# A masked attention stage with its values as the stationary operand, and spare products on PE ahead of two expert stages

## The chip, the cores and the metric

One core of a Trainium2 chip runs the whole program. The metric is the device time of one execution in microseconds (us), lower is better. Three executions of the kernel before took 1061.87, 1064.99 and 1067.60 us; their median is 1064.99 us.

## The reference

The input is 16 sequences of 128 tokens with 256 features, and a context tensor of the same shape. Four residual updates follow each other:

- `x += q + tril(c cT) q` with `q = layernorm(x)` and the context `c`, per sequence.
- A latent attention and a mixture of 8 experts. The tokens are normalized, brought down to 128 latent features, and split into 16 heads of 8 features. Rotated queries and keys give causal scores, and `attn = softmax(scores)`, `o = attn @ v`, `x + o @ w_up`. Each token then goes to 2 of 8 experts of width 512.
- A cross attention of 16 heads of 64 features, scaled by tanh of a gate.
- A mixture of 16 experts of width 256 (2 per token), and a shared expert of width 512 that all tokens use.

The change concerns the product `attn @ v` of the second item, with the division by the softmax's sums, and the beginnings of the two expert stages.

## The kernel before, in words

The kernel writes each engine's instructions in an order that a small planner fixes at build time. `latent_phases`, `expert_phases`, `cross_phases` and `shared_phases` (lines 161 to 360) declare phases: an engine, an assumed cost in ns, the phases that must come first, the PSUM banks that it holds, and a due time. `Plan.order` (lines 104 to 151) plays these costs forward and takes the phase whose start plus due is least; the table `LEAD` (lines 74 to 81) shifts single phases in it. The engines then run these orders in sequence, each instruction waiting for semaphores, so a phase that waits holds all that is behind it on its engine.

**The first stage** handles 16 blocks (one per sequence), pipelined over each other. For one block:

- PE forms the masked context product and applies it (`ctx`, `q1`), transposes the normalized tokens (`hnT`), and makes latent features (`c`) and queries, keys and values (`qkv`). ScalarE's `qkv_e` (line 998) copies the values into a ring of four tiles `v_`, each 16 heads times 9 columns. The ninth column of each head is a one, so that the product with the probabilities also gives their sum.
- `s` (line 701) writes scores of all 16 heads in four PSUM banks: a bfloat16 product that puts the causal mask there (line 708, 512 columns), then products of 32 rows (line 717) that lie in four different strips of the array.
- VectorE takes the maxima (line 1319), ScalarE the exponentials (line 1023), PE transposes the probabilities group by group (`pT`, line 727), ScalarE copies them out (`pT_e`, line 1030).
- `pv` (lines 730 to 738) multiplies: for each of the 16 heads the 128 by 128 transposed probabilities are the stationary operand, and the head's 9 value columns move.
- VectorE's `nrm0` (line 1322) takes reciprocals of the 16 sums per token and multiplies. The result has tokens on the partitions, so PE transposes it once more (`oT`, line 740), ScalarE copies it (`oT_e`, line 1032), and `up` (line 745) multiplies by `w_up`.
- The rest is a normalization and the router: transposes (`tT`), logits (`log`), counts (`cnt`) on PE, and small steps on VectorE (`ra`, `rb`), and GpSimd scatters the tokens to DRAM, sorted by expert (line 1780).

A float32 matmul appears in the profile as two LDWEIGHTS and MATMUL pairs, so the 16 products of `pv` are 32 records of each.

**The expert stages** (`r` = 0 and 1) walk over tiles of 128 sorted rows: SyncE loads a tile's rows (line 1863), `xT` (line 773) transposes them, `gate_up` (line 780) and `down` (line 796) multiply by the expert's weights. Before the first tile, SyncE and ScalarE write padding rows (lines 1845 and 1053 ff.). The first tile's `xT` waits for its rows, and PE with it.

Of the kernel before, what the change touches and what calls it, by code (L numbers as in the profile page):

```python
# [26 lines left out]
TRASH = 2 * NB * 128  # L27
KB = 256
# [12 lines left out]
def constants():  # L41
# [33 lines left out]
    "Q": 100, "SD": 600, "btg": 1000, "c_e": -100, "cpow": 800, "epow": 700, "exp0": -100, "ga0": 1200,  # L75
    "gates_a": -200, "gates_e": -1300, "kml": 1700, "kwl": -1600, "load_kv": -2400, "load_q": -700,
# [84 lines left out]
def latent_phases(p):  # L161
# [3 lines left out]
    for b in range(NB):  # L165
        def add(engine, ns, key, *after, banks=(), **kw):
            p.add(engine, ns, key, *after, banks=banks, due=20 * b, **kw)
# [15 lines left out]
        add("PE", 650, ("qkv", b), ("c_e", b), banks=[(misc, ("qkv_e", b))])  # L183
        add("ACT", 500, ("qkv_e", b), ("qkv", b), ("pv", b - 4), ("qkT", b - 2))
# [13 lines left out]
        add("PE", 3600, ("pv", b), *[(f"pT_e{g}", b) for g in range(4)], banks=[("pv", ("onrm", b))])  # L198
# [192 lines left out]
def program(nc, a, out):  # L391
    with ExitStack() as ctx:
# [96 lines left out]
        def emptied(*key, i=0):  # L489
            bk, n = USE[key][i]  # L490
            return freed[bk], n + 1
# [79 lines left out]
        o_ = lat.ring(2, 128)  # L571
        v_ = lat.ring(4, 16 * 9)
        rs_ = lat.ring(6, 8)
        sm_ = lat.ring(2, 64)
# [51 lines left out]
        def unit(s):  # L626

            return s // 8, s // 4 % 2, s // 2 % 2, s % 2

# [28 lines left out]
        def tensor(pe):  # L658
# [71 lines left out]
            def pv(b):  # L730
                vacant(pe, "pv", b)
                for g in range(4):
                    pe.wait_ge(*emptied(f"pT{g}", b))
                    for n in range(4):
                        h = 4 * g + n
                        i = pe.matmul(ps("pv", b)[:, h * 9:h * 9 + 9], pt_[g][:, n * 128:n * 128 + 128],  # L736
                                      v_[b % 4][:, h * 9:h * 9 + 9], start=True, stop=True)
                i.then_inc(*fills("pv", b))

            def oT(b):  # L740
                vacant(pe, "oT", b)
                pe.wait_ge(*emptied("pv", b))
                pe.transpose(ps("oT", b)[:, 0:128], o_[b % 2], ident).then_inc(*fills("oT", b))
# [195 lines left out]
            for phase, *at in ORDER["PE"]:  # L939
                if phase in ("pT0", "pT1", "pT2", "pT3"):  # L940
                    pT(at[0], int(phase[2]))
                elif phase == "EC":
                    cnt(at[0], 1)
                elif phase in ("gate", "up"):
                    gate_up(*at, phase)
                else:
                    {"ctx": ctx, "q1": q1, "hnT": hnT, "c": c, "qkv": qkv, "qkT": qkT, "s": s, "pv": pv, "oT": oT, "wup": up, "tT": tT,
                     "log": log, "cnt": cnt, "xT": xT, "down": down, "K": K, "V": V, "Q": Q, "S": scores, "T": T,
                     "PV": PV, "W": W, "NT": NT, "ET": ET, "EL": EL, "SG": SG, "SD": SD}[phase](*at)
# [25 lines left out]
        def scalar(act):  # L975
# [22 lines left out]
            def qkv_e(b):  # L998
                act.wait_ge(*full("qkv", b))
                if b >= 4:  # L1000
                    act.wait_ge(*full("pv", b - 4))
                v = v_[b % 4].rearrange("p (h d) -> p h d", d=9)
                if b < 4:
                    act.wait_ge(sem("sum_columns"), 4)
# [26 lines left out]

            def oT_e(b):
                act.wait_ge(*full("oT", b))
                if b >= 2:
                    act.wait_ge(*full("wup", b - 2))
                act.copy(oT_[b % 2], ps("oT", b)[:, 0:128]).then_inc(*frees("oT", b))
# [179 lines left out]
            for phase, *at in ORDER["ACT"]:  # L1216
# [4 lines left out]
                else:  # L1221
                    {"setup_a": setup, "hnT_e": hnT_e, "c_e": c_e, "qkv_e": qkv_e, "qkh": qkh, "oT_e": oT_e,
# [5 lines left out]
        def vector(v):  # L1228
# [4 lines left out]
            def setup():  # L1233
# [7 lines left out]
                for t in v_:  # L1241
                    v.memset(t.rearrange("p (h d) -> p h d", d=9)[:, :, 8:9], 1.0).then_inc(sem("sum_columns"), 1)
# [79 lines left out]
            def nrm0(b):  # L1322
                v.wait_ge(*full("pv", b))
                pv = ps("pv", b)[:, 0:144].rearrange("p (n d) -> p n d", n=16)
                sums = sm_[b % 2][:, 16:32].rearrange("p (n o) -> p n o", o=1)
                v.reciprocal(sums, pv[:, :, 8:9]).then_inc(dv, next_step("dve"))
                then()
                if b >= 2:
                    v.wait_ge(*full("oT", b - 2))
                v.tensor_tensor(o_[b % 2].rearrange("p (n d) -> p n d", n=16), pv[:, :, 0:8],  # L1330
                                sums.broadcast_to([128, 16, 8]), ALU.mult).then_inc(*frees("pv", b))
# [638 lines left out]
```

## Time and profile before

| | |
|---|---|
| median of three runs | 1064.99 us |
| the profiled execution, its own time | 1073.64 us |
| its span, first to last instruction | 1071.8 us |
| mean granted TensorE clock | 0.905 |
| busy: PE, its weight loads, DVE, ACT, POOL | 90%, 83%, 69%, 57%, 25% |
| first stage, from first to last `pv` | 53.7 to 254.1 us |
| first expert stage begins on PE | 281.3 us |
| second expert stage begins on PE | 876.6 us |

PE is the TensorE matmul, PEld its weight loads, DVE VectorE, ACT ScalarE, POOL GpSimd, SP SyncE. The granted clock is a share of full speed, where 0.50 is 1.2 GHz and 1.00 is 2.4 GHz.

### The profile page before, as it was taken

How to read it: one execution, taken by the hardware profiler on the slowest of the kernel's cores; microseconds unless marked ns; L12 is line 12 of the kernel's file. 1: busy time of each engine (PE TensorE's matmuls, PEld its weight loads, DVE VectorE, ACT ScalarE, POOL GpSimd, SP SyncE). 2: the span in 40 equal slices, each digit the busy share in tenths (PEclk: the TensorE clock that was granted, in tenths of full speed). 3: DMA queues.
4: the chain of work that ended last, by engine and by line, in shares of the span. 5: the costliest groups of instructions: out<-in, count | busy, mean ns of one | idle time of the engine just before them, and what ended most of it. 6: DMA issues, size and time to landing. Idle time of an engine off the chain costs nothing.

```text
span 1071.8 us, 23321 instructions
## 1 busy us (share of the span) xinstructions
PE 968.7 (90%) x7674; PEld 886.3 (83%) x7674; DVE 736.0 (69%) x2033; ACT 614.6 (57%) x1690; POOL 269.6 (25%) x323
## 2 busy tenths in 40 slices
PE   4799999997499999997899999999998829999994
PEld 3488888886499999996789899989887729999994
DVE  5876676654466776665899878576775528888836
ACT  1465666663366666666476486575775317767510
POOL 2544454543000000001735412101111103333300
PEclk7976787876699999998999999999998959999998
DMA  9600000000331111113111100000130853333242
GB/s 385 277 12 21 11 22 21 21 21 31 80 134 55 51 51 51 54 37 113 50 31 46 35 22 21 11 12 21 39 126 16 370 143 91 91 100 95 76 168 69
DMA packets 37317, 82.49 MB, mean 77 GB/s; under 512 B 5488, under 2 KB 28784, under 8 KB 35920
## 3 DMA queue, kind: packets, MB, share of 16 engines
q1 hardware_dynamic: 29760, 61.63, 16.6%
q0 software_dynamic: 6864, 18.85, 5.3%
q8 instruction: 63, 1.03, 0.4%
q10 hardware_dynamic: 576, 0.53, 0.2%
q14 instruction: 54, 0.44, 0.1%
HBM read 55.95 MB, written 25.04 MB: 76 GB/s over the span
## 4 chain that ended last, share of the span: by engine, by line
PE 76%; issue 6%; DVE 5%; DMA 4%; POOL 3%; ACT 2%; SPq 2%; ACTq 0%; DVEq 0%; another core or an unknown queue 0%; POOLq 0%
PE ps L792 17%; PE ps L654 8%; PE ps L656 8%; PE ps L655 8%; PE ps L736 6%; PE ps L727 4%; PE ps L877 3%; PE ps L856 3%; PE ps L866 3%; PE ps L935 2%; PE ps L708 2%; POOL yt_dram L1801 2%; PE ps L717 1%; DMA CT<-in_ctxT 1%; PE ps L692 1%
## 5 line engine op out<-in xcount | busy, mean ns | idle before, releaser
L654 PE MATMUL ps<-BIGR 128*128 128x256 f32 (+1 forms) x826 | 258.6, 313 | 7.6 <-DVE BIGR L1555 3.3
L792 PE MATMUL ps<-BIG 128*128 128x128 f32 x2000 | 254.5, 277 | 1.7 <-DVE BIG L1550 1.0
L792 PEld LDWEIGHTS ps<-BIG 128*128 128x128 f32 x2000 | 240.5, 194 | 3.5 <-DVE BIG L1550 2.4
L656 PE MATMUL ps<-BIGR 128*128 128x256 f32 x762 | 216.0, 283 | 0.0
L654 PEld LDWEIGHTS ps<-BIGR 128*128 128x128 f32 x826 | 158.5, 192 | 15.1 <-issue 9.3
L655 PE MATMUL ps<-BIGR 128*128 128x256 f32 (+1 forms) x570 | 168.9, 296 | 0.0
L656 PEld LDWEIGHTS ps<-BIGR 128*128 128x128 f32 x762 | 145.4, 191 | 0.0
L1080 ACT COPY BIG<-BIG 128x512 f32 (+1 forms) x86 | 70.1, 815 | 110.1 <-PE ps L792 73.9
L1543 DVE TENSOR_TENSOR BIGR<-BIG,BIGR 128x512 fp32r<-128x512 f32 (+1 forms) x86 | 80.4, 934 | 47.0 <-ACT BIGR L1089 46.8
L655 PEld LDWEIGHTS ps<-BIGR 128*128 128x128 f32 x570 | 109.2, 192 | 1.9
L1174 ACT ACTIVATE BIG<-ps,sm 128x128 f32<-128x128 f32 x256 | 91.5, 386 | 11.3 <-DVE sm L1644 11.1
L1793 POOL DMA_INDIRECT BIG<-ys_dram,YI x32 | 31.8, 994 | 238.1 <-DMA ys_dram<-BIG 230.4
L1780 POOL DMA_INDIRECT xs_dram<-TT,PI x64 | 65.2, 1018 | 95.7 <-DVE PI L1400 85.6
L1728 POOL TENSOR_TENSOR st<-st,CS 128x1 f32<-128x1 f32 (+1 forms) x64 | 43.4, 679 | 179.8 <-DVE st L1255 179.2
L1801 POOL DMA_INDIRECT yt_dram<-BIG,IX x47 | 48.8, 1039 | 123.1 <-DVE BIG L1563 120.7
L1089 ACT CAST BIGR<-BIG 128x512 fp32r (+1 forms) x86 | 69.4, 807 | 16.5 <-DMA BIG<-in_wd 11.1
L736 PEld LDWEIGHTS ps<-BIG 128*128 128x128 f32 x512 | 70.2, 223 | 3.3 <-issue 3.0
L655 PE MATMUL ps<-CTR,BIGR 128*128 128x256 f32 x256 | 72.9, 285 | 0.0
L736 PE MATMUL ps<-BIG 128*128 128x9 f32 x512 | 70.9, 280 | 1.8 <-ACT BIG L1030 1.5
L1550 DVE TENSOR_TENSOR BIG<-ps,BIG 128x256 f32<-128x256 f32 (+1 forms) x86 | 46.7, 543 | 34.2 <-PE ps L792 34.1
L1023 ACT ACTIVATE BIG<-ps,BIG 128x128 f32<-128x128 f32 x256 | 69.6, 432 | 0.0
L1641 DVE TENSOR_REDUCE sm<-ps 128x4 f32<-128x512 f32 x64 | 44.0, 687 | 32.0 <-PE ps L856 32.0
(221 smaller groups left out, 1998.5 us busy)
## 6 DMA issues: line engine op xcount, KB each, us to landing
BIG<-in_wd SPq DMA_DIRECT2D x2, 4096.0 KB, 35.5
BIG<-in_wgu SPq DMA_DIRECT2D x1, 6144.0 KB, 18.9
BIG<-xs_dram SPq DMA_DIRECT2D x47, 129.5 KB
BIG<-xs_dram SPq DMA_DIRECT2D x39, 128.0 KB
ys_dram<-BIG SPq DMA_DIRECT2D x39, 128.0 KB, 1.7
BIG<-yt_dram SPq DMA_DIRECT2D x16, 256.0 KB, 5.5
xs_dram<-zero SPq DMA_DIRECT2D x20, 129.5 KB, 7.1
X<-in_x SPq DMA_DIRECT2D x4, 512.0 KB, 8.6
```

The source lines that it names most:

```text
L654: pe.matmul(o, l[0], r[0], start=start, stop=False)
L655: pe.matmul(o, l[0], r[1], start=False, stop=False)
L656: return pe.matmul(o, l[1], r[0], start=False, stop=stop)
L736: i = pe.matmul(ps("pv", b)[:, h * 9:h * 9 + 9], pt_[g][:, n * 128:n * 128 + 128], v_[b % 4][:, h * 9:h * 9 + 9], start=True, stop=True)
L792: i = pe.matmul(o[:, c * 128:(c + 1) * 128], wt[:, at:at + 128], x[:, k * 128:(k + 1) * 128], start=k == 0, stop=k == 1)
L1023: i = act.activation(p_[g][:, at], ps("s", b, i=g)[:, at], ACT.Exp, bias=sm[:, 4 * g + n:4 * g + n + 1])
L1080: act.copy(W_[r][j % 2][:, n:2 * n], WGU[:, bass.ds(e * (2 * n) + n, n)]).then_inc(S["gu_upper"], 1)
L1089: act.copy(D_[j % len(D_)][:, 0:n], WD[:, bass.ds(e * n, n)]).then_inc(S["down_hi"], 1)
L1174: i = act.activation(xp_[s % 4][:, at], ps("S", s // 2, i=s % 2)[:, at], ACT.Exp, bias=sm[:, 4 + n:5 + n], accum_out=sm[:, 8 + n:9 + n])
L1543: v.tensor_tensor(wd[:, n:2 * n], WD[:, bass.ds(e * n, n)], wd[:, 0:n].bitcast(F32), ALU.subtract).then_inc(S["down_lo"], 1)
L1780: pool.indirect_dma_start(XS, bass.IndirectOffsetOnAxis(ap=PI[:, b, k:k + 1], axis=0), TT[tile_of(r, b)][:, :], None).then_inc(sem(f"scatt ...
L1801: pool.indirect_dma_start(YT, bass.IndirectOffsetOnAxis(ap=IX[:, j % 4:j % 4 + 1], axis=0), Y_[1][j % 3], None).then_inc(sem(f"results_pla ...
```

## The change

`pv` is turned round: a head group's values, padded to windows of 32 columns in which only one head's 8 columns are not zero, are the stationary operand, and the transposed probabilities move, 128 columns each. Four heads accumulate in one 32 by 128 piece of PSUM, and the four groups g lie at partitions 32g. A second set of 16 products has fixed tiles of ones as stationary operand and gives the sums, already spread over the partitions of each head. That makes 32 products for 16, all of form 128x32 with 128 moving columns, and the result comes out transposed, so `oT` and `oT_e` go. `nrm0` takes the reciprocal of 128 by 128 sums rather than of 128 by 16. `qkv_e` copies the values in four pieces. The ring of values has three tiles rather than four.

Before the first `xT` of the expert stages, PE does 40 (r = 0) and 24 (r = 1) bfloat16 products of 512 columns into the bank of `xT`, which then overwrites them. Assumed costs, some orderings and the table `LEAD` of the planner change as well, so the order of phases on every engine may change in all stages.

```diff
+VPAD = 88
+FILL = (40, 24)
 LEAD = {
-    "Q": 100, "SD": 600, "btg": 1000, "c_e": -100, ...
+    "ET_e": -300, "Q": 100, "SD": 600, "ah": -100, "btg": 1700, ...
-        add("PE", 650, ("qkv", b), ("c_e", b), banks=[(misc, ("qkv_e", b))])
-        add("ACT", 500, ("qkv_e", b), ("qkv", b), ("pv", b - 4), ("qkT", b - 2))
+        add("PE", 650, ("qkv", b), ("c_e", b), ("pv", b - 3), banks=[(misc, ("qkv_e", b))])
+        add("ACT", 600, ("qkv_e", b), ("qkv", b), ("pv", b - 3), ("qkT", b - 2))
-            add("PE", 440, (f"pT{g}", b), (f"exp{g}", b), banks=[("pT", (f"pT_e{g}", b))])
+            add("PE", 440, (f"pT{g}", b), (f"exp{g}", b), *[(f"pT{n}", b - 1) for n in range(4)], banks=[("pT", (f"pT_e{g}", b))])
-        add("PE", 3600, ("pv", b), ...)
-        add("DVE", 450, ("onrm", b), ("pv", b), ("oT", b - 2))
-        add("PE", 120, ("oT", b), ("onrm", b), banks=[(misc, ("oT_e", b))])
-        add("ACT", 170, ("oT_e", b), ("oT", b), ("wup", b - 2))
-        add("PE", 430, ("wup", b), ("oT_e", b), banks=[(misc, ("r", b))])
+        add("PE", 1800, ("pv", b), ...)
+        add("DVE", 560, ("onrm", b), ("pv", b), ("wup", b - 2))
+        add("PE", 430, ("wup", b), ("onrm", b), banks=[(misc, ("r", b))])
+        VAT, VWIN = (0, 48, 72, 32), (0, 40, 56, 8)
             def pv(b):
+
                 vacant(pe, "pv", b)
                 for g in range(4):
                     pe.wait_ge(*emptied(f"pT{g}", b))
+                if b == 0:
+                    pe.wait_ge(sem("sum_columns"), 8)
+                for x in range(2):
                     for n in range(4):
-                        h = 4 * g + n
-                        i = pe.matmul(ps("pv", b)[:, h * 9:h * 9 + 9], pt_[g][:, n * 128:n * 128 + 128],
-                                      v_[b % 4][:, h * 9:h * 9 + 9], start=True, stop=True)
+                        for g in range(4):
+                            w = v_[b % 3][:, VPAD * g:VPAD * g + VPAD] if x == 0 else ones_
+                            i = pe.matmul(ps("pv", b)[32 * g:32 * g + 32, 128 * x:128 * x + 128],
+                                          w[:, VWIN[n]:VWIN[n] + 32], pt_[g][:, n * 128:n * 128 + 128],
+                                          start=n == 0, stop=n == 3)
                 i.then_inc(*fills("pv", b))
-            def oT(b):
-                ...
             def up(b):
-                pe.wait_ge(*emptied("oT", b))
+                pe.wait_ge(*emptied("pv", b))
+            def keep_busy(bank, n):
+
+                for _ in range(n):
+                    pe.matmul(bank[:, :].rearrange("p (n t) -> p n t", n=4), identb[:, :],
+                              negb[:, :].rearrange("p (o t) -> p o t", o=1).broadcast_to([128, 4, 128]),
+                              start=True, stop=True)
             def xT(r, j):
                 vacant(pe, "xT", r, j)
+                if j == 0:
+                    keep_busy(ps("xT", r, j), FILL[r])
                 pe.wait_ge(sem(f"rows_loaded{j % 3}"), 16 * (rows_before(r, j) + 1))
             def qkv_e(b):
-                if b >= 4:
-                    act.wait_ge(*full("pv", b - 4))
-                v = v_[b % 4].rearrange("p (h d) -> p h d", d=9)
-                act.copy(v[:, :, 0:8], ps("qkv", b)[:, 256:384].rearrange("p (h d) -> p h d", d=8))
+                if b >= 3:
+                    act.wait_ge(*full("pv", b - 3))
+                else:
+                    act.wait_ge(sem("sum_columns"), 3)
+                v = v_[b % 3].rearrange("p (g c) -> p g c", g=4)
+                x = ps("qkv", b)[:, 256:384].rearrange("p (g n d) -> p g n d", g=4, n=4)
+                for n in range(4):
+                    act.copy(v[:, :, VAT[n]:VAT[n] + 8], x[:, :, n, :])
-            def oT_e(b):
-                ...
             def setup():
+                    v.memset(t, 0.0).then_inc(sem("sum_columns"), 1)
+                v.memset(ones_, 0.0).then_inc(sem("sum_columns"), 1)
+                ...
             def nrm0(b):
                 v.wait_ge(*full("pv", b))
-                v.reciprocal(sums, pv[:, :, 8:9]).then_inc(dv, next_step("dve"))
+                if b >= 2:
+                    v.wait_ge(*full("wup", b - 2))
+                o = oT_[b % 2]
+                v.reciprocal(o, ps("pv", b)[:, 128:256]).then_inc(dv, next_step("dve"))
                 then()
-                v.tensor_tensor(o_[b % 2]..., pv[:, :, 0:8], sums.broadcast_to([128, 16, 8]), ALU.mult)
+                v.tensor_tensor(o, ps("pv", b)[:, 0:128], o, ALU.mult).then_inc(*frees("pv", b))
```

## Rows read from the trace of the kernel before

**Rows 1.** The page: busy tenths, granted clock in 40 slices of the span

```profile
PE   4799999997499999997899999999998829999994
PEclk7976787876699999998999999999998959999998
```

**Rows 2.** Chain that ended last, share of the span by line

```profile
PE ps L792 17%; PE ps L654 8%; PE ps L656 8%; PE ps L655 8%; PE ps L736 6%; PE ps L727 4%; PE ps L877 3%; PE ps L856 3%; PE ps L866 3%; PE ps L935 2%; PE ps L708 2%; POOL yt_dram L1801 2%; PE ps L717 1%; DMA CT<-in_ctxT 1%; PE ps L692 1%
```

**Rows 3.** Stretches: us, busy of PE, PEld, DVE, ACT, POOL, granted clock, DMA share, GB/s

```profile
53.74:254.09 200.35, 197.90 (x1260) 168.14 (x1259) 133.10 (x437) 126.39 (x414) 89.62 (x117) 0.76 0.05 19
...
281.33:288.10 6.77, 6.26 (x28) 5.89 (x29) 0.00 (x0) 2.52 (x4) 0.00 (x0) 0.50 0.23 61
550.00:575.00 25.00, 24.83 (x238) 21.84 (x238) 23.40 (x64) 18.59 (x68) 10.68 (x13) 1.00 0.12 33
900.00:1000.00 100.00, 98.78 (x852) 96.85 (x850) 85.93 (x247) 71.29 (x177) 36.26 (x35) 1.00 0.32 96
...
876.60:882.10 5.50, 5.49 (x18) 4.78 (x19) 1.21 (x7) 0.37 (x1) 0.00 (x0) 0.51 0.17 50
```

**Rows 4.** Timeline of PE: start, us, group; a `pv`, and the last one

```profile
190.79 3.71 PE L736 MATMUL ps<-BIG 128*128 128x9 f32 x32
...
254.09 3.97 PE L736 MATMUL ps<-BIG 128*128 128x9 f32 x32
```

**Rows 5.** Timeline of PE: the cross attention's product of form 128x64

```profile
643.39 1.09 PE L877 MATMUL ps<-BIG 128*64 128x128 f32 x16
644.42 0.44 PE L866 MATMUL ps<-CS,BIG 128*128 128x128 f32 x2
```

**Rows 6.** Timeline of PE: products of 32 rows in four strips

```profile
200.79 0.97 PE L717 MATMUL ps<-BIGR 32*128 32x512 f32 x12
```

**Rows 7.** Reciprocals on VectorE, by line: duration ns min/median/max

```profile
L1649 DVE RECIPROCAL sm<-sm x64: 160/171/180, 534.9 to 820.1; 128x4 f32<-128x4 f32 x64
...
L1326 DVE RECIPROCAL BIG<-ps x16: 251/258/259, 58.2 to 258.1; 128x16 f32<-128x16 f32 x16
...
L1515 DVE RECIPROCAL GW<-GW x1: 352/352/352, 843.3 to 843.3; 128x32 f32<-128x32 f32 x1
```

**Rows 8.** Copies on ScalarE and the transpose that goes, by line

```profile
L1005 ACT COPY BIG<-ps x16: 245/265/293, 27.3 to 228.3; 128x128 f32<-128x128 f32 x16
...
L1036 ACT COPY BIG<-ps x16: 265/266/273, 63.4 to 259.3; 128x128 f32<-128x128 f32 x16
...
L743 PE MATMUL ps<-CS,BIG x16: 273/450/454, 63.1 to 258.8; 128*128 128x128 f32 x16
```

**Rows 9.** Chain in order of time and timeline: mask products, half and full clock

```profile
59.99 1.71 PE ps L708 x4
...
199.84 1.03 PE L708 MATMUL ps<-negb,identb 128*128 128x512 bf16 x4
```

**Rows 10.** Timeline of PE around the beginnings of the expert stages

```profile
268.17 0.17 PE L771 MATMUL ps<-mb,onesb 128*128 128x8 bf16 x1
281.33 0.45 PE L777 MATMUL ps<-CS,BIG 128*128 128x128 f32 x1 [12.99 <-DMA BIG<-xs_dram]
...
853.38 2.51 PE L935 MATMUL ps<-BIG,small 128*128 128x256 f32 x8 [2.55 <-DVE X L1702]
876.61 0.44 PE L777 MATMUL ps<-CS,BIG 128*128 128x128 f32 x1 [20.72 <-DMA BIG<-xs_dram]
```

**Rows 11.** Who waited, first stage: us in total, times, longest

```profile
POOL X L1768 <- DVE BIG L1339: 35.3, 13, 5.4
...
DVE BIG L1326 <- PE ps L736: 14.7, 13, 2.5
...
DVE BIG L1319 <- PE ps L717: 10.2, 9, 2.9
```

More of the change, by code:

```diff
@@ L74 @@
 LEAD = {
-    "Q": 100, "SD": 600, "btg": 1000, "c_e": -100, "cpow": 800, "epow": 700, "exp0": -100, "ga0": 1200,
-    "gates_a": -200, "gates_e": -1300, "kml": 1700, "kwl": -1600, "load_kv": -2400, "load_q": -700,
[4 rows of a table removed]
+    "ET_e": -300, "Q": 100, "SD": 600, "ah": -100, "btg": 1700, "c_e": 600, "cpow": 700, "epow": -700, "exp0": -100,
+    "ga0": 1300, "gates_a": -700, "kml": 200, "log": -300, "max": -3000, "max3": 100, "nh": -100, "nl": -200,
+    "owl": -1000, "pT0": 100, "pT3": -300, "pT_e0": -100, "pT_e1": 100, "pT_e3": -100, "pow3": -3700, "pro2": -300,
+    "qkT": -400, "qkh": -100, "qkl": -2200, "qkv_e": -200, "qw": 500, "qwl": 100, "r": -400, "ra1": -200,
+    "rope_p": 100, "route1": 1100, "sc0": 100, "sc1": -400, "sq": 700, "swh": -900, "tT": -1400, "tT_e": -100,
+    "te": 1500, "xbt": -100, "xh": 600, "xl": 100
 }
@@ L195, in latent_phases @@
             add("ACT", 1030, (f"exp{g}", b), (f"max{g}", b), (f"pT{g}", b - 1))
-            add("PE", 440, (f"pT{g}", b), (f"exp{g}", b), banks=[("pT", (f"pT_e{g}", b))])
+            add("PE", 440, (f"pT{g}", b), (f"exp{g}", b), *[(f"pT{n}", b - 1) for n in range(4)], banks=[("pT", (f"pT_e{g}", b))])
             add("ACT", 500, (f"pT_e{g}", b), (f"pT{g}", b), ("pv", b - 1))
-        add("PE", 3600, ("pv", b), *[(f"pT_e{g}", b) for g in range(4)], banks=[("pv", ("onrm", b))])
-        add("DVE", 450, ("onrm", b), ("pv", b), ("oT", b - 2))
-        add("PE", 120, ("oT", b), ("onrm", b), banks=[(misc, ("oT_e", b))])
-        add("ACT", 170, ("oT_e", b), ("oT", b), ("wup", b - 2))
-        add("PE", 430, ("wup", b), ("oT_e", b), banks=[(misc, ("r", b))])
+        add("PE", 1800, ("pv", b), *[(f"pT_e{g}", b) for g in range(4)], banks=[("pv", ("onrm", b))])
+        add("DVE", 560, ("onrm", b), ("pv", b), ("wup", b - 2))
+        add("PE", 430, ("wup", b), ("onrm", b), banks=[(misc, ("r", b))])
         add("DVE", 420, ("r", b), ("wup", b), ("xr", b - 2), ("tt", b - 2))
@@ L570, in program @@
         sq_ = lat.ring(1, D)
-        o_ = lat.ring(2, 128)
-        v_ = lat.ring(4, 16 * 9)
+        v_ = lat.ring(3, 4 * VPAD)
+        ones_ = lat.ring(1, VPAD)[0]
         rs_ = lat.ring(6, 8)
-        sm_ = lat.ring(2, 64)
+        sm_ = lat.ring(2, 16)
         ex0 = Space((120, BIGKB))
@@ L946, in tensor @@
                 else:
-                    {"ctx": ctx, "q1": q1, "hnT": hnT, "c": c, "qkv": qkv, "qkT": qkT, "s": s, "pv": pv, "oT": oT, "wup": up, "tT": tT,
+                    {"ctx": ctx, "q1": q1, "hnT": hnT, "c": c, "qkv": qkv, "qkT": qkT, "s": s, "pv": pv, "wup": up, "tT": tT,
                      "log": log, "cnt": cnt, "xT": xT, "down": down, "K": K, "V": V, "Q": Q, "S": scores, "T": T,
@@ L1030, in pT_e @@
                 act.copy(pt_[g], ps(f"pT{g}", b)[:, :]).then_inc(*frees(f"pT{g}", b))
-            def oT_e(b):
[L1033 to L1036, printed above, removed]
             def sq(b):
@@ L1221, in scalar @@
                 else:
-                    {"setup_a": setup, "hnT_e": hnT_e, "c_e": c_e, "qkv_e": qkv_e, "qkh": qkh, "oT_e": oT_e,
+                    {"setup_a": setup, "hnT_e": hnT_e, "c_e": c_e, "qkv_e": qkv_e, "qkh": qkh,
                      "sq": sq, "tT_e": tT_e, "pad_act": pad_act, "gates_e": gates_e, "wa": wa, "wdh": wdh, "xT_e": xT_e,
@@ L1241, in setup @@
                 for t in v_:
-                    v.memset(t.rearrange("p (h d) -> p h d", d=9)[:, :, 8:9], 1.0).then_inc(sem("sum_columns"), 1)
+                    v.memset(t, 0.0).then_inc(sem("sum_columns"), 1)
+                v.memset(ones_, 0.0).then_inc(sem("sum_columns"), 1)
+                v.wait_ge(sem("sum_columns"), 4)
+                for at in VAT:
+                    v.memset(ones_[:, at:at + 8], 1.0).then_inc(sem("sum_columns"), 1)
                 v.wait_ge(sem("consts_loaded"), 16)
@@ L1323, in nrm0 @@
                 v.wait_ge(*full("pv", b))
-                pv = ps("pv", b)[:, 0:144].rearrange("p (n d) -> p n d", n=16)
-                sums = sm_[b % 2][:, 16:32].rearrange("p (n o) -> p n o", o=1)
-                v.reciprocal(sums, pv[:, :, 8:9]).then_inc(dv, next_step("dve"))
+                if b >= 2:
+                    v.wait_ge(*full("wup", b - 2))
+                o = oT_[b % 2]
+                v.reciprocal(o, ps("pv", b)[:, 128:256]).then_inc(dv, next_step("dve"))
                 then()
[L1328 to L1331, printed above, removed]
+                v.tensor_tensor(o, ps("pv", b)[:, 0:128], o, ALU.mult).then_inc(*frees("pv", b))
             def r(b):
```

5 lines of the change are left out of this document (removed), and 4 rows, old and new, of the table LEAD.

## The prediction

> **What bounds the kernel now.** I read the page first. PE is busy nearly throughout, and its granted clock is at or close to full in the later stages but not in slices 2 to 11 [rows 1]. The chain that ended last is also mostly PE, and `pv`, line 736, has 6% of it [rows 2], some 64 us for 16 blocks of 9-column products. So the next view is the stretch from the first `pv` to the last: 200.35 us for 15 blocks, 13.36 us a block, with PE busy 197.90 us, or 99%, at a mean clock of 0.76, against DVE 133.10 and ACT 126.39 us [rows 3]. The reader should see two things there. PE alone sets the pace of the first stage. And it does so at a clock that is half of full for 48% of the time (0.76 is 0.52 at full and 0.48 at half). Freed of everything else, PE's work is 197.90 / 15 x 0.76 = 10.0 us of full clock a block; DVE's is 8.9 us, ACT's 8.4 us, POOL's 6.0 us. DVE waits for PE's products [rows 11], not the other way round. A faster `pv` is therefore worth its full price until DVE ends last, which is not far off.
>
> **`pv`.** Now 32 records take 3.71 us at mostly full clock [rows 4], about 112 ns each: with 9 moving columns that is the price of a 128-column weight load, not of a product. After, there are 64 records of 128 columns in a form with 32 weight columns. No row shows that form. The nearest is the cross attention's 128x64 form, whose products alternate between two halves of the array: 16 records in 1.09 us, of which the last one's latency of about 0.27 is tail, so 16 in about 0.87 [rows 5]. That is 54 ns a record, half of 112, so two column strips do work side by side. Four strips by rows do too: 12 records of 512 columns in 0.97 us [rows 6], where one after another they would need 12 x 0.217 = 2.6 (0.217 per 512 columns, from (1.03 - 0.38) / 3, the mask products at full clock [rows 9]). The changed loop runs g innermost, so each product goes to another strip than the last. I take four strips side by side: 64 / 4 x 109 ns = 1.75 us, and 0.15 for starting, 1.9 us. The bounds are 1.75 and, if no strip overlaps, 64 x 109 = 7.0 us; 54 ns, as the row of two strips has it, gives 3.5. I take the lowest but for the start because both rows of strips show the full factor that their number allows. `oT` takes one more product of 0.11 us at full clock off PE. PE's work becomes 10.0 - 3.6 + 1.9 - 0.1 = 8.2 us of full clock a block.
>
> The Trainium skill (TensorEngine Tiling (Array Packing), Key Properties) speaks against this: changing the tiling mode drains the engine. Behind the 64-column products of this trace the next one starts 1.03 us after they began [rows 5], some 0.1 to 0.2 us later than without a gap; by the page with such a drain at both ends of 16 `pv` it would be at most 6 us of PE in all, in a stage where PE is then no longer last, so the sum stays.
>
> **The clock.** Half clock comes in each block now, in the stretches with `pv` and behind it, where the array moves 9 columns per weight load. After, `pv` moves 128 columns in four strips, and 8.2 us of dense work would lie in some 11 us. I take the clock as close to full, 0.93 or more. If it keeps falling, that is a rival.
>
> **DVE.** The reciprocal grows from 16 to 128 elements per partition. Between 4 and 32 elements it costs (352 - 171) / 28 = 6.5 ns an element, and 258 ns at 16 [rows 7]; so 258 + 112 x 6.5 = 0.98 us, 0.72 more a block. Its bounds are 0.3 (no dependence on size) and 1.2 us. The planner assumes 560 ns for the pair, which I do not follow. The multiplication has 128 x 128 elements before and after. DVE's work becomes 133.10 / 15 + 0.72 = 9.6 us a block. It is now the largest of all, so DVE ends last. What share can it reach? At its best it is busy 23.40 of 25 us, and over a long PE-bound stretch 85.93 of 100 [rows 3]. That gives 9.6 / 0.94 = 10.2 and 9.6 / 0.86 = 11.2 us a block. I take 11.2: the order of phases is laid out with a too small `onrm`, and PE and ACT are then at 73 to 80% too.
>
> **ACT.** Four copies of 128x32 for one of 128x128 in `qkv_e`: each between 0.20 and 0.265 [rows 8], so 0.5 to 0.8 us more, less 0.27 for `oT_e` [rows 8]: 8.8 us a block at most. Hidden behind DVE; if DVE were faster it would be next. The other edits cost nothing: the zeroing of the tiles in the setup lies behind the first loads; `qkv_e` waits for the `pv` of three blocks back, `nrm0` for the `wup` of two back, both a whole block early; and `pv` waiting for all four `pT_e` costs its pipeline at most the copy of one group, 0.6 us of latency, against the 0.7 us that `oT` with `oT_e` give back.
>
> **Sum of the first stage.** 15 x (13.36 - 11.2) = 32 us. Behind the last `pv` the stage is a chain of dependent steps: that `pv` itself shrinks from 3.97 us [rows 4] to about 2 us, `oT` with its copy goes, the longer reciprocal comes: 2 us more. Together 34 us.
>
> **The 40 products.** PE stands idle 12.99 us, from 268.3 until the first rows land, and then works at clock 0.50 for 6.77 us [rows 3, 10]. The idle is set by DMA and the queues that pad, which the products do not touch. One product costs 1.71 / 4 = 0.43 us at half and 0.217 at full clock [rows 9]. The clock rose after 5.5 and 6.8 us of work in the two stage beginnings [rows 3], so 13 to 16 products run at half and the rest at full: 11.3 to 12.0 us. They end a microsecond before the rows; if the clock does not rise they take 17.2 us and delay the stage by 4. Then the expert stage's first 6.77 us run at full clock and take about half: 3 us gained, with bounds from 4 lost to 3.4 gained.
>
> **The 24 products.** The last product ahead of the second stage ends at 855.9, the rows land at 876.6 [rows 10]. 24 products take 5.2 us at full and 10.3 at half clock, so they end by 866, and more than 10 us of idle follow, as in front of the first stage, where such an idle left the clock at half. I expect nothing from them, neither gain nor loss, and the 5.50 us at 0.51 [rows 3] stay.
>
> **The new orders** of the later stages I count as 0, between 4 us gained and 5 lost: PE is at 98% there already [rows 3]. Together -32 - 2 - 3 = -37 us: the profiled span of 1071.8 would become 1035, its time 1073.64 about 1037. It stands 8.65 us above the median of the runs, so from the median, 1064.99 - 37 = 1028 us.
>
> **Rivals.** A difference within 0.5%, 5 us, is no difference here.
>
> *The clock keeps falling.* The 16 transposes a block and the small router products stay, and between them PE now waits for DVE. With the mean clock still at 0.76, PE needs 8.2 / 0.76 = 10.8 us a block, on top of DVE's 9.6; two engines so close give 12 us: -20 - 2 - 3, 1040 us. For it: the half-clock share is now 48%. Against: what held the clock down was mostly `pv`. The Trainium skill (TensorE: Matmul & The Clock Gate, Part 4) says that transposes do not count as busy for the clock, which would make this case likelier.
>
> *The 64 pairs are paced by their issue.* A pair of weight load and product every 105 ns is what the densest stretch shows (238 in 25 us [rows 3]), though those are long products. By that bound `pv` takes 6.7 us, PE 13.0 at full clock, and the time falls only by 5 + 3: 1057 us. A short burst goes faster, 54 ns [rows 5], which gives 3.5 us, PE 9.8, DVE still last, about 1032. In between, 1040. The Trainium skill (same page, Back-to-back issue gap) gives about 81 ns for such pairs; by it `pv` would take 5.2 us, PE 11.5, and the time would be near 1038.
>
> *No strip overlaps* (the slower case). `pv` then takes 7.0 us of full clock, PE 10.0 - 3.6 + 7.0 - 0.1 = 13.3, already all of the present 13.36. With the clock at 0.9, since transposes and waits still lower it a little, it is 14.8 us a block: 15 x 1.4 = 21 us lost, 3 won back by the 40 products, 1083 us. It decides from a `pv` of about 6 us on. Against it stand both strip rows.
>
> *The stage is faster, the program is not.* What the first stage gains, an order in the later stages loses. That needs over 30 us there, where PE idles little.
>
> **How the numbers follow.** Forecast 0.60, clock falls 0.17, issue 0.13, lost later or nothing gained 0.05, slower 0.05. The first three are all faster by more than 0.5%: 0.90; within 0.5%: 0.05; slower: 0.05. The range: DVE at 94% gives 15 x 3.2 = 47 + 5, 1013, and 3 from the orders 1010; at the other end 12.4 us a block with nothing for the tail gives 1050. 1010 to 1050 leaves out the slower case and the worst of the issue case.
>
> **What would show it.** Right: 64 records of `pv` in about 2 us, spaced near 27 ns; reciprocals near 1 us; blocks 11.2 us apart; clock above 0.9 in the first stage; DVE busy 86% there; PE idle in it for the first time, waiting for DVE; first expert stage at clock 1.00 from its first product; second one still at half. Wrong: `pv` records 109 ns apart, a clock of 0.76 as now, a reciprocal of 0.3 us (then below 1015), or PE still at 99%.

## The result and the profile after

The changed kernel takes 1020.41 us (median of 4 runs, 1019.6 to 1025.98) against 1065.72 us of the kernel before: ratio 0.959, 95% interval 0.9547 to 0.9634. That is 45 us or 4.1% faster, inside the range of 1010 to 1050 and 8 us below the forecast of 1028. Its profiled execution has a span of 1018.3 us and a time of 1020.09 us.

The page of the changed kernel, its busy tenths and the granted clock, answers to [rows 1]:

```profile
PE   4788888878999999978999999999999759999994
PEclk7889999998999999988999999999999979999997
```

PE is now below 9 in slices 3 to 9 where it stood at 9, and the clock is at 9 in slices 4 to 9 where it moved between 6 and 8. The chain of the changed kernel answers to [rows 2]; the first stage's product, now line 744, has 2% of it, and two VectorE lines appear:

```profile
PE ps L805 18%; PE ps L657 9%; PE ps L659 9%; PE ps L658 9%; PE ps L869 3%; PE ps L890 3%; PE ps L879 3%; PE ps L948 2%; POOL yt_dram L1812 2%; PE ps L744 2%; PE ps L730 1%; DVE BIG L1340 1%; DMA CT<-in_ctxT 1%; PE ps L711 1%; DVE BIG L1332 1%
```

Stretches of the changed kernel, with the columns of [rows 3]: first to last `pv`, the first expert stage's first 6.8 us, the cross attention from the first expert stage's last gate to the last count, and the second expert stage's first 5 us:

```profile
51.70:219.70 168.00, 142.24 (x1735) 101.48 (x1735) 145.81 (x450) 123.82 (x445) 90.66 (x123) 0.97 0.07 22
243.60:250.40 6.80, 6.29 (x54) 6.08 (x55) 1.38 (x2) 3.68 (x6) 0.00 (x0) 1.00 0.30 79
445.30:791.60 346.30, 331.28 (x2931) 298.85 (x2930) 260.83 (x780) 231.29 (x771) 97.77 (x110) 0.98 0.15 51
826.00:831.00 5.00, 5.00 (x20) 4.28 (x21) 0.80 (x4) 0.37 (x1) 0.00 (x0) 0.59 0.19 52
```

The first line is the heart of it: 15 blocks in 168.00 us, 11.2 us each, at a clock of 0.97, with DVE busy 145.81 us, 87%. The time before split by stages, from the two profiled executions:

| stage | before, us | after, us | difference |
|---|---|---|---|
| start to the first `pv` | 53.7 | 51.7 | -2.0 |
| first `pv` to the last | 200.4 | 168.0 | -32.4 |
| last `pv` to the first expert stage | 27.2 | 23.9 | -3.3 |
| first expert stage, to its last gate product | 204.7 | 201.7 | -3.0 |
| cross attention, to the last count | 355.0 | 346.3 | -8.7 |
| to the second expert stage's first product | 35.6 | 34.4 | -1.2 |
| second expert stage and end | 195.2 | 192.3 | -2.9 |

Together -53.5 us, from a profiled execution of before that lay 8 us above the median. The split is that of two single executions; stages of the same code differ by some us from one profile to the next, as the experiments show.

The timeline of PE in the changed kernel shows one `pv`, and the last one:

```profile
148.51 1.95 PE L744 MATMUL ps<-BIG 128*32 128x128 f32 x64
...
219.67 1.95 PE L744 MATMUL ps<-BIG 128*32 128x128 f32 x64 [0.49 <-ACT BIG L1045]
```

64 records in 1.95 us, in all 16 blocks alike. Four records start within 20 ns, the next four 134 ns behind them, and every further four 109 ns behind the last, so about 16 x 109 ns and a tail. The reciprocal of the changed kernel, by line, answers to [rows 7]:

```profile
L1340 DVE RECIPROCAL BIG<-ps x16: 939/952/958, 53.7 to 221.7; 128x128 f32<-128x128 f32 x16
```

And around the first expert stage, where [rows 10] had 12.99 us of idle:

```profile
230.47 11.62 PE L780 MATMUL ps<-negb,identb 128*128 128x512 bf16 x40
243.59 0.33 PE L790 MATMUL ps<-CS,BIG 128*128 128x128 f32 x1 [1.50 <-DMA BIG<-xs_dram]
...
805.80 5.34 PE L780 MATMUL ps<-negb,identb 128*128 128x512 bf16 x24
825.96 0.48 PE L790 MATMUL ps<-CS,BIG 128*128 128x128 f32 x1 [14.82 <-DMA BIG<-xs_dram]
```

The 40 end 1.50 us before the rows; behind the 24 there are 14.82 us of idle.

### The profile page after: what moved, and what is told of

Read it like the earlier page. It is cut to its first block, busy times and chain, and to the rows that moved or that the text cites. A ratio compares the mean times of both kernels' runs of the same rounds, so it can differ in the third digit from the quotient of the medians.

```text
span 1018.3 us, 24462 instructions
## 1 busy us (share of the span) xinstructions
PE 915.6 (90%) x8234; PEld 816.4 (80%) x8234; DVE 748.7 (74%) x2037; ACT 610.0 (60%) x1722; POOL 266.4 (26%) x323
## 4 chain that ended last, share of the span: by engine, by line
PE 68%; DVE 12%; issue 8%; DMA 4%; POOL 3%; SPq 2%; ACT 2%; ACTq 1%; DVEq 0%; POOLq 0%
PE ps L805 18%; PE ps L657 9%; PE ps L659 9%; PE ps L658 9%; PE ps L869 3%; PE ps L890 3%; PE ps L879 3%; PE ps L948 2%; POOL yt_dram L1812 2%; PE ps L744 2%; PE ps L730 1%; DVE BIG L1340 1%; DMA CT<-in_ctxT 1%; PE ps L711 1%; DVE BIG L1332 1%
## 5 line engine op out<-in xcount | busy, mean ns | idle before, releaser
L805 PE MATMUL ps<-BIG 128*128 128x128 f32 x2000 | 251.0, 275 | 1.4 <-DVE BIG L1561 0.9
L805 PEld LDWEIGHTS ps<-BIG 128*128 128x128 f32 x2000 | 237.4, 192 | 2.3 <-DVE BIG L1561 1.4
L1804 POOL DMA_INDIRECT BIG<-ys_dram,YI x32 | 32.4, 1013 | 234.3 <-DMA ys_dram<-BIG 226.6
L1739 POOL TENSOR_TENSOR st<-st,CS 128x1 f32<-128x1 f32 (+1 forms) x64 | 42.9, 672 | 168.3 <-DVE st L1268 167.9
L1098 ACT CAST BIGR<-BIG 128x512 fp32r (+1 forms) x86 | 69.4, 807 | 15.8 <-DMA BIG<-in_wd 10.4
L1038 ACT ACTIVATE BIG<-ps,BIG 128x128 f32<-128x128 f32 x256 | 71.8, 414 | 10.6 <-DVE BIG L1332 10.6
L1183 ACT ACTIVATION_READ_ACCUMULATOR BIG<-ps,sm 128x1 f32 x256 | 57.4, 224 | 0.0
L1547 DVE COPY BIG<-BIG 128x512 f32 (+1 forms) x86 | 47.2, 549 | 11.0 <-issue 3.5
## 6 DMA issues: line engine op xcount, KB each, us to landing
BIG<-in_wd SPq DMA_DIRECT2D x2, 4096.0 KB, 34.4
```

Of the source, the lines that this page charges most:

```text
L805: i = pe.matmul(o[:, c * 128:(c + 1) * 128], wt[:, at:at + 128], x[:, k * 128:(k + 1) * 128], start=k == 0, stop=k == 1)
L1038: i = act.activation(p_[g][:, at], ps("s", b, i=g)[:, at], ACT.Exp, bias=sm[:, 4 * g + n:4 * g + n + 1])
L1098: act.copy(D_[j % len(D_)][:, 0:n], WD[:, bass.ds(e * n, n)]).then_inc(S["down_hi"], 1)
L1183: i = act.activation(xp_[s % 4][:, at], ps("S", s // 2, i=s % 2)[:, at], ACT.Exp, bias=sm[:, 4 + n:5 + n], accum_out=sm[:, 8 + n:9 + n])
L1547: v.tensor_copy(W_[r_][j % 2][:, 0:n], WGU[:, bass.ds(e * (2 * n), n)]).then_inc(S["gu_lower"], 1)
```

## The experiments

Stage lengths come from each run's profile, since one stage disturbs the totals: the second expert stage, between its first and its last row transpose, took 128.7 to 137.7 us in kernels that are the same there (see the last section). The first stage is the same code in the changed kernel's two profiles and in those of experiments 3 and 8, and took 168.0, 167.9, 171.0 and 165.9 us from the first to the last `pv`: a difference of up to 5 us there need not be the effect of an edit.

**1. No strip side by side.** The loop over groups goes outside, all else stays.

```diff
-                for x in range(2):
-                    for n in range(4):
-                        for g in range(4):
+                for g in range(4):
+                    for x in range(2):
+                        for n in range(4):
```

> The changed kernel, with the loop over the four groups outermost in pv, so that 16 products in a row lie in the same column strip. If strips side by side make pv short: the 64 records come 109 ns apart, pv takes 7.0 us instead of 1.9, PE has 13.3 us of full clock a block again, blocks come 13.4 to 14 us apart instead of 11.2, and the time rises by 30 to 45 us, to 1050 to 1065. If the engine finds the overlap itself, or pv is off the path: pv stays at 1.9 us or the time stays within 5 us of 1020.

Measured: 1088.09 us, ratio to before 1.0188 (1.0107 to 1.0268), more than the 1050 to 1065 expected. A `pv` of this kernel in the timeline of PE:

```profile
162.23 5.93 PE L744 MATMUL ps<-BIG 128*32 128x128 f32 x64
```

And the stretch of its first stage, columns as in [rows 3]:

```profile
52.10:276.00 223.90, 201.31 (x1731) 161.91 (x1731) 146.48 (x448) 125.54 (x444) 90.77 (x123) 0.98 0.05 17
```

Within a strip the records come 109 ns apart; only at the three changes of strip do the first records of the next one run beside the last four or so of the old, which makes 5.93 us of the expected 7.0. Blocks come 14.9 us apart, more than the expected 14: PE is busy only 90% of the stage, since VectorE now waits for `pv` (54.9 us in total) in an order laid out for a short one. So the slower rival was real in its mechanism and close in its price (5.93 us for its 7.0, 14.9 us a block for its 14.8, 1088 us for its 1083), and what decides is the order of three loops.

**2. The kernel before, with a wider moving operand and nothing else.** Weight loads, products and their order stay; each product moves its 9 columns seven times over. (`nrm0` reads its columns at the new spacing; that line is not shown.)

```diff
-                        i = pe.matmul(ps("pv", b)[:, h * 9:h * 9 + 9], pt_[g][:, n * 128:n * 128 + 128],
-                                      v_[b % 4][:, h * 9:h * 9 + 9], start=True, stop=True)
+                        i = pe.matmul(ps("pv", b)[:, h * 28:h * 28 + 63].rearrange("p (o d) -> p o d", o=7),
+                                      pt_[g][:, n * 128:n * 128 + 128],
+                                      v_[b % 4][:, h * 9:h * 9 + 9].rearrange("p (o d) -> p o d", o=1).broadcast_to([128, 7, 9]),
+                                      start=True, stop=True)
```

> The kernel before, with one thing changed: pv's 9 moving columns are read seven times over, 63 moving columns, of which the first 9 are used (heads lie 28 columns apart in the bank). A record was paced by its 128-column weight load, 112 ns, so at full clock pv should take 3.6 us as before. If the low clock of the first stage comes from the array moving so little in pv: the clock there rises from 0.76 to 0.9 or more, blocks come 10.5 to 11.5 us apart instead of 13.4, and the time falls by 28 to 40 us, to 1025 to 1038, with none of the change made. If the gain was the cycles that pv lost and the clock followed from something else: clock 0.76, time within 5 us of 1065, or longer if the wider products cost more.

Measured: 1036.18 us, ratio 0.9707 (0.9631 to 0.9782), 34.6 us below the kernel before on the same chip. The stretch of its first stage:

```profile
54.80:217.30 162.50, 157.29 (x1260) 128.46 (x1260) 134.36 (x439) 123.75 (x414) 90.03 (x117) 1.00 0.07 23
```

And one `pv` in its timeline of PE:

```profile
108.91 3.68 PE L736 MATMUL ps<-BIG 128*128 128x63 f32 x32
```

This is the main finding. `pv` takes 3.68 us, as long as a full-clock `pv` before (3.71 us [rows 4]), but the clock stays at 1.00 through the stage where it was 0.76, and blocks come 10.83 us apart. Its first expert stage starts at 243.4 us, that of the changed kernel at 243.6. A wider operand that computes nothing new gives the whole gain of the first stage, and values stationary, in the order that it has here, gives nothing beyond it.

**3. No products ahead of the expert stages.** `FILL = (0, 0)`.

> The changed kernel without the 40 and 24 products. If the 40 hold the clock for the first expert stage and the 24 do nothing: the first expert stage starts at clock 0.50 for 5 to 7 us, its last gate comes 3 us later after its first row, the second stage is unchanged, time +3, 1023.5. If both do nothing: 1020.

Measured: 1039.06 us, ratio 0.9743 (0.9666 to 0.982), so 14 to 19 us above the changed kernel (experiment 6 and the result) instead of the expected 3. The first expert stage's first 6.8 us are

```profile
248.60:255.40 6.80, 6.28 (x32) 5.92 (x33) 0.00 (x0) 2.52 (x4) 0.00 (x0) 0.57 0.20 57
```

with 32 records of PE where the changed kernel's first profile has 54, and the stage takes 204.2 us to its last gate against 201.7: 2.5 us for the 40 products in that profile, as expected (experiment 6 has another profile, in which they gave nothing). Of the rest, 5 us lie ahead of the stage (11.4 us a block), 1.7 in the cross attention, 0.6 behind it, and 9 in the second expert stage: 137.7 against 128.7 us, with eleven waits of VectorE for the landing of scattered results. The 5 us lie in code that the edit does not touch, and within the spread given above. What makes the 9 us is not shown: three other kernels have as long a second expert stage with or without products ahead of it (136.0 to 137.3 us), but all four runs of this one lie between 1038.19 and 1041.52 us, so an effect of the edit is not ruled out.

**4. A short reciprocal.**

```diff
-                v.reciprocal(o, ps("pv", b)[:, 128:256]).then_inc(dv, next_step("dve"))
+                v.reciprocal(o[:, 0:16], ps("pv", b)[:, 128:144]).then_inc(dv, next_step("dve"))
...
-                v.tensor_tensor(o, ps("pv", b)[:, 0:128], o, ALU.mult).then_inc(*frees("pv", b))
+                v.tensor_tensor(o, ps("pv", b)[:, 0:128], cst["triu"], ALU.mult).then_inc(*frees("pv", b))
```

> The changed kernel with a reciprocal of 16 instead of 128 columns in nrm0, and the product taken with a constant instead, so the attention is not divided by its sums. DVE has 0.7 us less a block. If DVE's work sets the first stage's pace: blocks 10.5 us apart instead of 11.2, time -8 to -11, 1010 to 1012. If it is the latency of chains between engines, or PE: less than 3 us.

Measured: 1026.19 us (1020.96 to 1033.58), ratio 0.9607 (0.9511 to 0.9703), where the profiled run, 1031.33 us, has 137.3 us in the second expert stage. The first stage:

```profile
51.80:218.30 166.50, 144.32 (x1735) 101.66 (x1737) 136.16 (x449) 123.59 (x445) 91.41 (x123) 0.97 0.07 23
```

DVE has 9.65 us less to do, and the stage is 1.5 us shorter, which is within its spread: 11.1 for 11.2 us a block. DVE's load does not by itself set the pace. The chain that ended last does change: between the first and the last `pv` of the changed kernel the reciprocal has 7.2% of it (12.1 us). Here the reciprocal is not among its larger parts, and ScalarE's exponentials have 8.0%.

**5. The reciprocal twice**, in the same order of phases.

```diff
                 v.reciprocal(o, ps("pv", b)[:, 128:256]).then_inc(dv, next_step("dve"))
                 then()
+                v.reciprocal(o, ps("pv", b)[:, 128:256]).then_inc(dv, next_step("dve"))
+                then()
```

> The changed kernel with the 128x128 reciprocal done twice, 0.98 us more of DVE a block, in the same order. If DVE's work set the pace, as forecast: 0.98 us a block, 15 us, 1038 to 1040. If, as short_recip says, it does not (0.73 us less gave 0.1 us a block): a few us at most as far as the step lies in a chain, up to 1030.

Measured: 1058.88 us (10 runs), ratio 0.989 (0.9853 to 0.9926). The first stage:

```profile
52.90:246.50 193.60, 154.03 (x1731) 110.62 (x1730) 160.14 (x464) 125.84 (x444) 91.07 (x123) 0.90 0.06 19
```

12.9 us a block, 1.7 more for 0.96 more of DVE. Neither theory: more than DVE-bound, although DVE is busy 83% only. The clock has fallen from 0.97 to 0.90. The reciprocal stands in the way from `pv` to `up` of the same block, and PE waits there (line 752) for the steps of `nrm0`:

```profile
PE ps L752 <- DVE BIG L1344: 16.2, 11, 2.1
```

16.2 us in 11 waits, where the changed kernel has 5.6 in 9 and experiment 4 has 0.9 in 2. So one more of these steps costs at least its full length, and a shorter one gains little, since the chain then runs by another way (experiment 4). That the waits and the lower clock together make the 1.7 us is argued, not isolated.

**6. The changed kernel again**, as base for the next three.

> The changed kernel once more, on the chip and in the rounds of the three that follow, as their base: 1020, or up to 10 us more if the second expert stage, whose length was 128.7 us in one profile of this kernel and 137 us in two of its near relatives, varies with the chip's DRAM and not with the kernel.

Measured: 1024.95 us (1022.11 to 1027.28), ratio 0.9626 (0.9589 to 0.9663). The blocks' distances repeat those of the first profile almost to 0.1 us (9.6, 13.8, 16.2, 8.8, 15.5 and so on, where the other had 9.6, 13.8, 16.1, 8.8, 15.5). That speaks for a fixed order, but not against an engine at its limit: the PE-bound kernels of experiments 2 and 10 repeat theirs as well (8.3, 10.9, 10.4, 12.8, 11.7).

This profile has something that the first one did not show. The timeline of PE around the first expert stage, and the stretch of the stage's first 6.8 us:

```profile
230.66 10.09 PE L780 MATMUL ps<-negb,identb 128*128 128x512 bf16 x40
244.12 0.47 PE L790 MATMUL ps<-CS,BIG 128*128 128x128 f32 x1 [3.37 <-DMA BIG<-xs_dram]
...
244.10:250.90 6.80, 6.27 (x30) 5.91 (x31) 0.00 (x0) 2.52 (x4) 0.00 (x0) 0.54 0.24 60
```

The same 40 products ran more of their time at full clock and ended 3.37 us before the rows. The stage's first 6.8 us had a clock of 0.54 and 30 records, and it took 204.4 us to its last gate: next to nothing gained. In the ten profiles with the 40 products, they ended 1.3 to 1.5 us before the rows three times (the first profile, experiments 4 and 9), and there the clock was 1.00 in the stage's first 6.8 us and the stage took 201.7 us. Seven times they ended 2.0 to 3.4 us before them; there the clock was 0.51 to 0.75 and the stage took 203.1 to 204.7 us, against 204.0 to 204.7 in the four profiles without them. These are different kernels; no run varies the idle time alone.

**7. The old LEAD table in the changed kernel.**

> The changed kernel with the LEAD table of before. If the table is worth something: the stretch from the first expert stage's end to the last count of the cross attention goes from 346 back to 353 to 355 us, as in both kernels with the old table, and the time rises by 5 to 10 us. If the orders do not matter: that stretch stays at 346 to 350.

Measured: 1043.13 us, ratio 0.9787 (0.9743 to 0.9831), 18 us above experiment 6. The cross attention went to 349.7 us from 345.1. By the expectation's bounds that still speaks for "the orders do not matter" there; against its own base it is 4.6 us, hardly more than the spread. The larger part was not foreseen: the first stage has 11.9 us a block, with one distance of 25.6 us, and its first `pv` comes 2.8 us later. At equal products and nearly equal clock (0.96), an order alone is worth 10.7 us between the first and the last `pv`, more than the spread of that stage.

**8. 90 products ahead of the second expert stage.** `FILL = (40, 90)`.

> The changed kernel with 90 instead of 24 products ahead of the second expert stage. 90 last 19.5 us at full clock, from about 806 to 825.5 us, just up to the rows at 826. If the clock at the stage's beginning is worth what it was in the first one: the 4 to 5 us of half clock there go, the first tiles come 2 to 3 us earlier, time -2 to -3. If that beginning is bound by something else (GpSimd's scatters, the shared expert): 0. If the products run past the rows: slower by what they run over.

Measured: 1024.35 us, ratio 0.962 (0.9577 to 0.9663), the same as experiment 6. The timeline of PE of this kernel:

```profile
807.33 19.59 PE L780 MATMUL ps<-negb,identb 128*128 128x512 bf16 x90
826.81 0.33 PE L790 MATMUL ps<-CS,BIG 128*128 128x128 f32 x1
```

And the stretch behind it:

```profile
826.80:832.00 5.20, 5.20 (x40) 4.99 (x40) 1.94 (x9) 1.37 (x4) 0.00 (x0) 1.00 0.24 68
```

The clock is 1.00 from the first product on, and PE has 40 records in 5.2 us where the changed kernel's first profile has 20 in 5.0. Yet the stage is no shorter: 129.6 us to its last row transpose, 129.2 in experiment 6. That beginning is not bound by PE.

**9. One of DVE's steps on GpSimd.**

```diff
-        add("DVE", 650, ("hn", b), ("pow2", b), ("hnT", b - 2), ("r", b - 5))
+        add("DVE", 420, ("hn", b), ("pow2", b), ("hnT", b - 2))
+        add("POOL", 750, ("hp", b), ("pow2", b), ("r", b - 5))
...
+            def hp(b):
+                s = st[:, 8 + b % 8, :]
+                pool.wait_ge(*done("pow2", b))
+                if b >= 5:
+                    pool.wait_ge(*emptied("wup", b - 5))
+                pool.tensor_scalar(h_[b % 5], X[:, b, :], s[:, 6:7], s[:, 8:9], ALU.subtract,
+                                   ALU.mult).then_inc(S["h_ready"], 1)
```

> The changed kernel with one of DVE's steps of each first-stage block (the normalized residual, 0.48 us) moved to GpSimd, which is busy 6 of 11 us. If DVE's work sets the pace: blocks come 0.4 to 0.5 us closer together, 10.7 us, time -6 to -8. If it is the order and the waits between engines: within 3 us, or slower, as GpSimd takes about 0.7 us and others wait behind it.

Measured: 1044.96 us, ratio 0.9799 (0.9749 to 0.9849), 20 us above experiment 6; 12.7 us a block. The step costs GpSimd far more than I took (groups of GpSimd, busy us and mean ns):

```profile
L1755 POOL TENSOR_SCALAR BIG<-X,st 128x256 f32<-128x256 f32 x11 | 14.1, 1278 | 0.4
```

1.28 us for what DVE does in about 0.41. The planner also put many other phases elsewhere, and the square on ScalarE also waits for the one before, so this run mixes a dear step with another order and separates neither.

**10 to 12. Without values stationary.** Three kernels on the base of before. `wide_cross` is experiment 2 with the 40 and 24 products and these values of the new table:

```diff
+    "btg": 1700, "cpow": 700, "epow": -700, "ga0": 1300, "max": -3000, "pro2": -300, "qw": 500, "ra1": -200,
+    "sc1": -400, "swh": -900, "te": 1500, "ET_e": -300, "ah": -100, "qwl": 100, "xbt": -100
```

and without the old table's `gates_e`, `kwl`, `load_kv`, `load_q`, `load_shared`, `load_w1`, `ss` and `tanh`.

> The kernel before with 63 moving columns in pv (as in wide_pv), the 40 and 24 products, and the changed LEAD values of the cross attention and the shared expert alone; no values stationary. If the clock, the 40 products and the orders are the whole gain: first stage as in wide_pv, 10.8 us a block; 2.5 to 3 us less in the first expert stage; 4 to 7 us less in the cross attention; 1036 - 3 - 5 = 1028, between 1024 and 1032, near the changed kernel's 1020 to 1025. If values stationary is worth something of its own: no nearer than 1032.

Measured: 1029.23 us, ratio 0.9643 (0.955 to 0.9736). First stage:

```profile
55.90:218.30 162.40, 157.26 (x1260) 128.44 (x1258) 134.34 (x439) 123.72 (x414) 89.85 (x117) 1.00 0.07 23
```

10.83 us a block again, 348.4 us of cross attention (352.6 in experiment 2). The first expert stage takes 203.4 us (204.0 there), less than the 2.5 to 3 us expected of the products, which here ended 2.04 us before the rows and left the clock at 0.75 in the stage's first 6.8 us. The changed kernel's ratios, 0.959 and 0.9626, lie within its interval: no difference between the two kernels is shown.

`wide_newlead` has the whole new table. Its ScalarE squares also wait for the one before, since they share a scratch tile.

> As wide_cross, but with the changed kernel's whole LEAD table, which was made for the other form of pv. If the table suits a kernel only as a whole and with its own costs: the first stage has over 11.3 us a block and the time is above wide_cross's, 1030 to 1045. If it is good in itself: the first stage is at 10.8 or less, 1020 to 1028.

Measured: 1054.3 us, ratio 0.9876 (0.9785 to 0.9967): 12.8 us a block, with distances of 21.3 and 25.1 us among them and a clock of 0.93. That is even more than the 1030 to 1045 expected for a table that suits only its own kernel: as a whole it does harm with this form of `pv`. How much of the loss comes from the added wait is not separated.

`new_lead_only` is the kernel before with that table and the same wait.

> The kernel before with the changed LEAD table alone. If the orders of the cross attention carry over: 4 to 8 us less between the first expert stage's end and the last count. The first stage stays PE-bound at clock 0.76 with 13.4 us a block, or gets worse by the table made for another pv. Time 1055 to 1075; if the table were the main cause of the gain, below 1045.

Measured: 1093.35 us, ratio 1.0242 (1.0144 to 1.0341). Clock 0.76 and 15.0 us a block; the cross attention took 347.6 us against 355.0, the expected gain. That was above the expected 1075, for the first stage lost more than allowed for.

## Why the prediction was right, and where its reasons were not

**`pv`: right.** 64 records in 1.95 us for 1.9 forecast, four strips side by side. The next product starts 0.20 us behind the start of the last record, where it is 0.11 us in experiment 2, so a change of form costs some 0.1 us. By the Trainium skill's figure of about 81 ns a pair (TensorE: Matmul & The Clock Gate, Back-to-back issue gap) an estimate would be 5.2 us; the trace does not agree, 64 pairs come within 1.95 us. The issue rival is thereby out.

**The clock: right, and underrated.** 0.97 for 0.93 or more. But the prediction counted the clock and PE's cycles as one sum and let DVE cap it. Experiment 2 shows what each is worth: the clock alone takes 13.36 to 10.83 us a block, and the 1.7 us that `pv` then still loses cost the stage nothing against the changed kernel. The rival "the clock keeps falling" is out too: it stayed up although the 16 transposes a block remain.

**PE's work: mis-sized.** The forecast had 8.2 us of full clock a block; 142.24 / 15 x 0.97 is 9.2. The 10.0 us for the kernel before was too low already: experiment 2, at a clock of 1.00, has 157.29 / 15 = 10.5. Why busy time at a mixed clock gives too little is not shown. It did no harm, since PE did not end last.

**DVE ends last: the step that failed.** The 0.98 us for the reciprocal was right (0.95), the 11.2 us a block came out to the digit, and DVE's share is 87% for the 86% assumed. Yet 9.65 us less work in DVE moved the stage by 1.5 us (experiment 4), and experiment 2's kernel, with 8.96 us of DVE a block, is PE-bound at 97%. The 11.2 us belong to chains that go from engine to engine in the planned order: a doubled reciprocal costs 25.6 us in the stage, a shortened one gives 1.5 us, and another order alone costs 10.7 us (experiments 5, 4 and 7). That the two numbers met is luck. An engine's busy share of 87% was read as its limit; taking work away from it tells.

**The tail: right in kind,** -3.3 us for -2. **The start,** -2.0 us, was not in the sum. It may hang on the table, since with the old one the first `pv` comes at 53.7 to 55.9 us and with the new one at 50.9 to 52.9 us, but for experiment 8, which has the new one and 54.4.

**The 40 products: right in one profile, and partly by luck.** 11.62 us for 11.3 to 12.0, ending 1.50 us before the rows; 2.5 to 3.0 us gained for 3. In the second profile of the same kernel they ended 3.37 us before the rows and gained nothing, and over ten profiles the whole gain came three times (experiment 6). The forecast named only one way to lose it, that the clock does not rise; what happened is that it rose early, the products ended sooner, and it had fallen again when the rows came or soon behind. **The 24: right,** the stage still begins mostly at half clock (0.59 in its first 5 us). Experiment 8 adds that even a held clock brings nothing there.

**The orders: mis-sized.** The forecast had 0, between 4 gained and 5 lost. The cross attention is 8.7 us shorter in the two profiles; over all kernels of this study it took 349.7 to 355.0 us in three profiles with the old table and 345.1 to 351.3 in eleven with the new values, so the table is worth about 5 us in the mean, and the two ranges overlap a little. "PE is at 98% there already" came from the stretch of an expert stage; the cross attention itself had PE at 334.49 of 355.0 us, 94%, which the rows did not show. With the 2 us of the start and 1.3 us of the tail this is an estimate of the 8 us by which the forecast was too high; it mixes profiles with medians and is no closer than a few us.

## What to carry to other kernels

Look at what the low clock of a stage costs before removing products: here a stage that was PE-bound and half of its time at half clock was freed by moving 63 columns per weight load for 9, at no cost in time, since the load was the longer part. A busy share near 90% does not show that an engine sets the pace; take a piece of its work away, or double it, and see. Products whose only use is to hold the clock ahead of a wait held it here in three profiles of ten: look at the clock behind them in more than one. In a statically ordered kernel a table of priorities belongs to the durations it was made with: moved whole to the other form, it cost 25 us against the part of it for the later stages (with one more wait on ScalarE).

## What the runs showed of the hardware that was not expected

- 63 moving columns cost no more than 9 behind a 128-column float32 weight load (3.68 and 3.71 us for 32 records), and the granted clock stayed at 1.00 where it averaged 0.76.
- The same 40 products took 11.62 us in one profile and 10.09 in another of the same kernel, and the clock behind them was 1.00 after 1.50 us of idle and 0.54 after 3.37 us.
- Products in different column strips overlap even when the strips are not interleaved: at each change of strip some four records run beside the last of the strip before, 5.93 us for 64 records where 109 ns each would be 7.0.
- A GpSimd step of 128x256 with two per-partition scalars takes 1.28 us, against 0.41 for the same step on VectorE and 0.73 to 0.76 for a product or a sum of two tiles of that size on GpSimd.
- The second expert stage, the same but for the products ahead of it, took 128.7 to 137.7 us from its first to its last row transpose. Where it is long, VectorE waits for scattered results to land; the waits in the kernel of experiment 3 and, from another view (idle time before the instruction), in the changed one:

```profile
DVE PL L1510 <- DMA yt_dram<-BIG,IX: 16.3, 11, 2.0
```

```profile
L1510 DVE SCALAR_TENSOR_TENSOR PL<-BIG,TE 128x1 f32<-128x1 f32 x46 | 9.9, 215 | 4.0 <-DMA yt_dram<-BIG,IX 3.9
```

16.3 us of waits in the one, 3.9 in the other. Over all profiles these waits are 13.4 to 16.3 us where the stage took 134 us or more and 3.5 to 10.5 us where it took less. Nothing tried here says what makes the landing slow; it hits kernels of before and after alike. It is a part of the spread of some 10 us in their times.
